# Hyperbolic hops of a graph network in blocks of 64 tiles, with two half chains on VectorE and one set of head buffers

## What is computed

```python
    def _agg(entity_emb, relation_emb, head, tail, relation_type):
        head_emb = entity_emb[head]
        tail_emb = entity_emb[tail]
        rel_emb = relation_emb[relation_type]
        ricci = _l2_normalize(tail_emb + rel_emb)
        hyper_head = expmap0(head_emb)
        hyper_tail = expmap(tail_emb, hyper_head)
        hyper_rel = expmap(rel_emb, hyper_head)
        res = project(mobius_add(hyper_tail, hyper_rel))
        res = logmap(res, hyper_head) + ricci * 1e-07
        res = jax.nn.relu(res)
        sums = jnp.zeros((n_entities, res.shape[-1]), res.dtype).at[head].add(res)
        ...
    for _ in range(N_HOPS):
        e = _agg(e, relation_emb, head, tail, relation_type)
        e = _l2_normalize(e)
        entity_res_emb = RES_LAMBDA * entity_res_emb + e
```

## Time and profile before

| | |
|---|---|
| median of 3 runs | 24083.2 us (24078.12 to 24092.08) |
| the profiled execution | 24039.33 us, its span 24037.5 us |
| first hop, and second hop with the end | from about 16471 us; from about 20276 us |
| VectorE busy, of the span | 16546.3 us (69%) |
| GpSimd busy, of the span | 12605.7 us (52%) |

### The profile page before, as it was taken

One profiled execution on the slowest core, in us unless ns is written; L12 is line 12 of the kernel. 1 busy time (PEld: TensorE's weight loads), 2 busy tenths in 40 slices (PEclk: granted clock), 3 DMA queues, 4 the chain that ended last, 5 costly groups with the idle time before them and its releaser, 6 DMA issues. The chain is left out here.

```text
span 24037.5 us, 205919 instructions
## 1 busy us (share of the span) xinstructions
PE 10326.4 (43%) x47565; PEld 6860.3 (29%) x47566; DVE 16546.3 (69%) x26071; ACT 2139.0 (9%) x3670; POOL 12605.7 (52%) x12782
## 2 busy tenths in 40 slices
PE   0033326655555555556666422222333333333333
PEld 0033322222222222222222322222333332333332
DVE  8744439988888888886666211115888886878887
ACT  0011110000000000000000000001111111111111
POOL 0188876655566555536665166653444443444443
PEclk9999997555555555558887555555555555555555
DMA  4133331111111111121112001113111112111112
GB/s 170 25 69 69 69 64 25 24 23 23 22 21 23 23 23 23 22 20 24 24 24 23 9 21 21 21 21 49 52 51 50 51 50 41 52 51 50 52 50 42
DMA packets 1118452, 942.42 MB, mean 39 GB/s; under 512 B 775931, under 2 KB 887579, under 8 KB 1117875
## 3 DMA queue, kind: packets, MB, share of 16 engines
q0 software_dynamic: 419904, 437.84, 9.9%
q1 hardware_dynamic: 698096, 500.67, 8.0%
HBM read 726.46 MB, written 207.32 MB: 39 GB/s over the span
## 5 line engine op out<-in xcount | busy, mean ns | idle before, releaser
L1420 POOL DMA_INDIRECT tail<-ball,h_idx x3328 | 3271.7, 983 | 1793.3 <-issue 1231.1
L736 PE MATMUL p_rad<-w_stack,hid_t 99*128 99x512 bf16 (+1 forms) x6656 | 3079.6, 620 | 2391.3 <-DVEq L826 1161.0
L808 DVE TENSOR_REDUCE red<-prod 128x96 f32<-128x1536 f32 x1664 | 2898.3, 1742 | 3.5
L1098 POOL DMA_INDIRECT l_xg<-h_tab,l_idx x1664 | 1571.2, 944 | 1444.1 <-issue 828.3
L1452 PE MATMUL h_sum<-head,h_hot 128*128 128x64 f32 x6656 | 1444.2, 421 | 1987.4 <-ACT head L1498 1987.4
L1438 PE MATMUL h_head<-ball_parts,hot_t 128*128 x9984 | 1067.6, 281 | 2813.4 <-issue 1578.1
L337 POOL DMA_INDIRECT rec_a<-rec,slot x1600 | 1990.4, 1244 | 517.2 <-issue 500.5
L692 POOL DMA_INDIRECT rec_b<-l_rcb x1600 | 1920.0, 1200 | 571.6 <-issue 570.5
L930 POOL DMA_INDIRECT l_xg<-x_tab,l_idx x1664 | 1571.6, 944 | 1141.8 <-issue 874.0
L946 PE MATMUL l_sum<-outer,l_hot 128*128 128x512 f32 x3328 | 1693.3, 673 | 945.6 <-DVEq L991 869.7
L736 PEld LDWEIGHTS p_rad<-w_stack,hid_t 99*128 99x128 bf16 (+1 forms) x6656 | 774.5, 132 | 4337.7 <-issue 4336.0
(11 more groups left out here) (369 smaller groups left out, 18896.7 us busy)
## 6 DMA issues: line engine op xcount, KB each, us to landing
hot_t<-rows_l SPq DMA_DIRECT2D x208, 512.0 KB
rec_a<-fill SPq DMA_DIRECT2D x128, 728.0 KB, 19.6
l_rec<-rec_a SPq DMA_DIRECT2D x104, 896.0 KB, 4.8
rhot_t<-rows_r SPq DMA_DIRECT2D x208, 384.0 KB
tail<-ball,h_idx POOLq DMA_INDIRECT x3328
t<-in_type SPq DMA_DIRECT2D x100, 500.0 KB
l_xg<-in_x,l_idx POOLq DMA_INDIRECT x1664
l_xg<-x_tab,l_idx POOLq DMA_INDIRECT x1664
```

Source lines behind the costliest of these rows:

```text
L736: ins = pe.matmul(p_rad[j % 2][:, h * 512:(h + 1) * 512], hid_t[j // 4 % 2][0:K3 + 3 * (1 - i), j % 4, i, :], w_stack[i][0:K3 + 3 * (1 - i ...
L808: ch.step(dve.tensor_reduce(red[:, j, :], prod[j % 3][:, :, :], AX, ALU.add))
L1420: pool.indirect_dma_start(tg[q][:, j, :], None, table[:, :], bass.IndirectOffsetOnAxis(ap=idx[q][:, j:j + 1], axis=0)).then_inc(gathered[q ...
```

## The change

A block becomes 64 tiles (`W` = `HU * BT`, four units of 16), so a hop has 26 blocks. On VectorE each operation of the chain is written twice, once per half block of 32 tiles, and waits for the operation before last instead of the last. To make room, `head`, `rel` and `t_dot_r` are held once instead of twice, the one-hot of the sum is two buffers of 8 tiles, `p_rel` is one bank, and the lists of nodes, lanes and relations go to DRAM and come back block by block. Therefore TensorE picks the heads of block b+1 after the sums of block b; the map words are read during the sums (`words`). ScalarE signals each copy by itself. GpSimd gathers a unit as soon as that unit is released. Outside the hops, `x_kept` is stored in `norm_phase` and read back, the halved entity sum goes through DRAM between the hops (`ent_kept`), and the semaphores of two earlier phases are shared and cleared at their end.

```diff
+HU = 4
...
-        W, Q, H = 2 * BT, BT // 2, BT // 4
+        W, Q, H, N2 = HU * BT, HU * BT // 4, BT // 4, HU * BT // 2
+        HP8 = BT // 2
...
-        hg = [sb(f"head{q}" + tag, [P, W, T_PICK]) for q in range(2)]
-        rg = [sb(f"rel{q}" + tag, [P, W, D + 2]) for q in range(2)]
+        hg = sb("head" + tag, [P, W, T_PICK])
+        rg = sb("rel" + tag, [P, W, D + 2])
...
+            def rows(b, u):
+                h = u % 2
+                hold(sp, turn, picked, (b * HU + u) * H + (AHEAD - H))
...
+            def body(b, q, it, left):
+                rows(b, 0)
+                rows(b, 1)
+                if left:
+                    hold(sp, turn, tails_read, b + 1)
+                    lists(b + 1, 1 - q)
+                    hold(sp, turn, ends_used, b + 1)
+                    edge_ends(b + 1, 1 - q)
+                rows(b, 2)
+                rows(b, 3)
...
-                    hold(pool, turn, tails_used, b + 1)
-                    ch.do(pool.tensor_copy(idx[q][:, :], g["dst_b"][:, bass.ds(b * W, W)]))
+                    hold(pool, turn, idx_in[q], it * 16 + 16)
                     for j in range(W):
+                        if j % BT == 0:
+                            hold(pool, turn, tails_used, b * HU + (j // BT + 1))
...
             def body(b, q, it, left):
-                if left:
-                    pick(b + 1)
                 hold(pe, turn, added, b + 1)
+                chunk = []
                 for j in range(W):
                     if j % BT == 0:
...
+                        if left:
+                            chunk.extend(words(b + 1, j // BT))
+                        hold(pe, turn, relu_done, b * HU + (j // BT + 1))
+                    if j % HP8 == 0:
+                        hold(pe, turn, edge_hot, b * (2 * HU) + (j // HP8 + 1))
+                    ins = pe.matmul(p_sum[:, j // 2, :], hot[j // HP8 % 2][:, j % HP8, :], hg[:, j, 0:D], start=(j % 2 == 0), stop=(j % 2 == 1))
+                    if j % HP8 == HP8 - 1:
                         ins.then_inc(sum_done, 1)
+                if left:
+                    pick(b + 1, chunk)
...
-                act.wait_ge(copied, 2)
-                act.sem_clear(copied)
-                act.sem_inc(taken, 1)
+            def quads(b):
+                for k in range(Q):
+                    hold(act, turn, picked, b * Q + (k + 1 + AHEAD))
+                    act.activation(rg[:, 4 * k:4 * k + 4, :], p_rel[:, :, 0:D + 2], ACT.Copy).then_inc(rel_taken, 1)
+                    act.activation(hg[:, 4 * k:4 * k + 4, :], p_head[k % 2][:, :, 0:T_PICK], ACT.Copy).then_inc(taken, 1)
...
+            def hots(q, b, m):
+
+                z = slice(m * HP8, m * HP8 + HP8)
+                if m >= 2:
+                    dve.wait_ge(sum_done, b * (2 * HU) + (m - 1))
...
-                    z = slice(0, W)
...
-                    ch.sync()
-                    ch.step(f(S, S2, E, B2, z))
+                    for half in range(2):
+                        z = slice(half * (W // 2), (half + 1) * (W // 2))
...
+                        if ch.n > 1:
+                            dve.wait_ge(chain_s, ch.n - 1)
+                        ch.step(f(S, S2, E, B2, z))
...
-                hots(q, b, 0)
+                if left:
+                    compares(b + 1, 0)
+                    compares(b + 1, 1)
...
-                hots(q, b, 1)
+                if left:
+                    relation_hots(1 - q, it + q)
...
+                    for m in range(2):
+                        hots(q, b, 2 * u + m)
+                dve.sem_inc(ends_used, 1)
+                for u in range(HU):
+                    dve.wait_ge(sum_done, b * (2 * HU) + (2 * u + 2))
+                    add_groups(dve, ch, chunk[u * BG:u * BG + BG], acc, lambda k: p_sum[:, u * BG + k:u * BG + k + 1, :])
+                dve.sem_inc(added, 1)
                 if left:
-                    tails(1 - q, b + 1, it + q)
-                    heads(1 - q, b + 1, load_chunks)
...
+                    compares(b + 1, 2)
+                    tails(1 - q, it + q)
+                    compares(b + 1, 3)
+                    heads(1 - q, b + 1)
...
-            store_nodes(sp, x_kept, g["x"], D, stored)
+            w = NT // list_i.shape[1]
+            sp.dma_start(list_i, g["dst_b"][:, :].rearrange("p (b w) -> p b w", w=w)).then_inc(stored, 16)
...
-            norm_phase(nc, g, acc, g["dis"], None, "2", bias=bias)
+            norm_phase(nc, g, acc, g["dis"], x_kept, "2", bias=bias)
...
+            load_phase(nc, tab[:, :, 0:D], x_kept, "0")
```

More of the change, by code:

```diff
@@ L1083, in spread_phase @@
         gathered = [sem(f"l2_gathered{u}") for u in range(4)]
-        row_ready, idx_ready, hot_done, sum_done, added, turn, chain_s = (
-            sem("l2_" + n) for n in ("row_ready", "idx_ready", "hot_done", "sum_done", "added", "turn", "chain"))
+        both = shared(g, ["h_" + n for n in ("row_ready", "idx_ready", "hot_done", "sum_done", "added", "turn", "chain")])
+        row_ready, idx_ready, hot_done, sum_done, added, turn, chain_s = both
+        ctx.callback(clear_shared, nc, both)
         block = ctx.enter_context(nc.Block())
@@ new lines, in pick @@
+            def pick(b, chunk):
+                for k in range(Q):
+                    u, i = k // H, k % H
+                    if i == 0:
+                        hold(pe, turn, hot_done, b * HU + (u + 1))
+                    hold(pe, turn, taken, b * Q + (k + 1))
+                    for j in range(4):
+                        for part in range(3):
+                            pe.matmul(p_head[k % 2][:, j, 0:T_PICK], hot_t[u % 2][:, 4 * i + j, :],
+                                      parts[:, bass.ds(chunk[2 * k + j // 2], 1), part, :], start=(part == 0), stop=(part == 2))
+                    hold(pe, turn, rel_taken, b * Q + (k + 1))
+                    for j in range(4):
+                        ins = pe.matmul(p_rel[:, j, 0:D + 2], rhot_t[u % 2][:, 4 * i + j, :], rel_parts[:, :], start=True, stop=True)
+                    ins.then_inc(picked, 1)
@@ L1454, in body @@
                         ins.then_inc(sum_done, 1)
+                if left:
+                    pick(b + 1, chunk)
             pe.sem_inc(picked, AHEAD)
-            pe.sem_inc(sum_done, SEED)
-            pick(0)
+            pick(0, [c for u in range(HU) for c in words(0, u)])
             all_blocks(pe, NW, body)
@@ L1500, in _ @@
             act.activation(p_row[:, 0:P], g["row"][:, :], ACT.Copy).then_inc(row_ready, 1)
             act.sem_inc(taken, SEED)
-            for k in range(Q):
-                quad(0, 0, k)
+            act.sem_inc(rel_taken, 1)
+            quads(0)
             all_blocks(act, NW, body)
@@ new lines, in with_relation, with tails, heads @@
+            def with_relation(vec, out, u):
+                ch.do(tt(v2[:, :, 0:NREL3], vec[:, unit(u), T_REL:T_REL + NREL3], rhot[:, unit(u), :], MUL_))
+                ch.do(dve.tensor_reduce(out[:, unit(u)], v2[:, :, 0:NREL3], AX, ADD))
+            def tails(q, it):
+                dve.wait_ge(gathered[q], it * (16 * W) + 16 * W)
+                for u in range(HU):
+                    with_relation(tg[q], tr, u)
+                dve.sem_inc(tails_read, 1)
+            def heads(q, b):
+                t = tg[q]
+                for u in range(HU):
+                    z = unit(u)
+                    dve.wait_ge(taken, b * Q + ((u + 1) * H + SEED))
+                    with_relation(hg, sc[:, HV + 1, :], u)
+                    ch.do(tt(v2[:, :, :], hg[:, z, 0:D], t[:, z, 0:D], MUL_))
+                    ch.do(dve.tensor_reduce(sc[:, HV, z], v2[:, :, :], AX, ADD))
+                dve.wait_ge(rel_taken, b * Q + (Q + 1))
@@ L1700, in body, with load_chunks @@
                 big = [P, BT, D]
-                for half in range(2):
-                    z = slice(half * BT, half * BT + BT)
+                chunk = []
+                def load_chunks():
+                    chunk.extend(chunks(dve, g["map"][1], b * (N2 // PACK) + len(chunk) // PACK))
+                for u in range(HU):
+                    z = unit(u)
                     for vec, c in ((h, 16), (t, 18), (r, 19)):
                         ch.step(tt(vec[:, z, 0:D], vec[:, z, 0:D], bc(sc[:, c, z].unsqueeze(2), big), MUL_))
+                    load_chunks()
@@ L1727, in body, with unit_phase @@
                 ch.restart()
-                dve.sem_inc(added, 1)
-            compares(0)
-            tails(0, 0, 0)
+            for u in range(HU):
+                compares(0, u)
+            relation_hots(0, 0)
+            tails(0, 0)
             heads(0, 0)
-            compares(1)
             ch.restart()
             all_blocks(dve, NW, body)
-def unit_phase(nc, g, acc, ent, tab, tag):
+def unit_phase(nc, g, acc, ent, ent_from, ent_to, tab, tag):
     with ExitStack() as ctx:
```

284 lines of the change are left out of this document (127 added, 157 removed).

## The result

The changed kernel took 23944.1 us (median of 4 runs, 23927.7 to 23970.5) beside 24087.6 us of the kernel before: a ratio of 0.994, 95% interval 0.9923 to 0.9958. It is 143 us faster, where 628 were forecast, and lies outside the range. Later sets of runs fell on other chips, and there the same two kernels stood at 0.9587 (0.9571 to 0.9603), 974 us apart, outside the range on its other side. What follows explains both.

What follows compares the result with a forecast made beforehand. VectorE was taken to set the hops' pace: 114.4 us of work plus 11.9 of waiting make 126.3 per 64-tile block, 3372 per hop against 3698. Saving 652 in both hops, less 24 around them, gives 23455 us, range 23120 to 23845.

Steps and rivals of the forecast that it cites:

- Chain: VectorE's chain of dependent operations as two streams: 32.0 us per 64 tiles, the second stream saving 23.7 us.
- Rival 1: In VectorE's chain, two streams gain nothing: a block of 150.0 us, 24689 us in all; chance 7%.
- gaps inside the loop: Extra time of VectorE's chain inside the loop over outside it: 3.2 us per 64 tiles, bounds 0 and 5.
- Rest of VectorE's row: VectorE's work outside the chain per 64 tiles, including vector products 24.6, additions 12.0, heads 16.4 and tails 5.8 us.
- Ends of a hop, and around: First chain 132 us after the hop's start, last block 83 us; stores, loads and semaphore clearing around the hops +24 us.
- The wait that comes in: After the additions VectorE waits 11.9 us per block for rows that need TensorE's picks, now made after its sums.
- R: The moment in a block when VectorE finishes the last unit's vectors, from which the wait for picks is counted.
- lower bound of 6: Shortest wait for picked rows per block, 6 us, with sums ending early, no late copy and no table load.
- no further wait: After the first wait for rows, VectorE finds unit 3's rows and heads ready, with 5 us to spare.
- idle times of 0 or 24 us: Sign in the profile: VectorE idle this long before a block's second L1552, instead of some 12 us, refutes the hand-over sum.
- rival 2: The hand-over of picks costs twice as much, 24 us a block, ScalarE being late: 138.3 us, total 24057; chance 3%.
- its half, 132 to 137 us: Half the extra hand-over cost: a block of 132 to 137 us, 23750 to 24000 us in all; chance 10%.

Runs made afterwards that it cites:

- e18: The changed kernel, unaltered, run again on a chip with signals on time: 22570.0 us, 0.9586 of the kernel before.
- e4: Changed kernel with each chain operation waiting for the one just before it instead of the last but one: 23678.4 us, 1.0057 of the kernel before.
- e7: The kernel before, unaltered, profiled on a chip with signals on time: 23555.0 us (one run).
- e5: The changed kernel, unaltered, on a chip with signals on time: 22580.7 us, 0.9587 of the kernel before.
- sets 3 and 4: Two sets of follow-up runs, each on its own chip, with late signals; the kernel before took 24060.0 and 24040.2 us there.
- e11: The kernel before with four additional ScalarE copies ahead of each quad's copies, as a delay: 24234.7 us, 1.0075 of the unaltered kernel before.
- sets 1, 2 and 5: Three sets of follow-up runs, each on its own chip, with signals on time; the kernel before took 23545.2, 23554.9 and 23541.4 us.
- e15: Changed kernel with the gathers of tails left out in both hops, on a chip with late signals: 22741.1 us (one run).

## Why the prediction was wrong, step by step

From one block of each profile (e18 from 17546.30 on, the first profile from 18008.87 on), and the hops:

| term, us | forecast | on time (e18) | late (first profile) |
|---|---|---|---|
| chain with two comparisons and relation one-hot | 37.9 | 35.1 | 34.2 |
| vectors, words, eight one-hots | 37.4 | 37.0 | 37.3 |
| additions | 12.0 | 11.8 | 11.7 |
| waits for picks | 11.9 | 5.3 | 15.2 + 6.0 + 6.5 |
| comparisons, tails, heads, trip of the loop | 27.1 | 29.3 | 26.3 |
| period, mean of 25 | 126.3 | 117.0 | 136.4 |
| start of the hop to the first chain | 132 | 128.9 | 126.9 |
| last body | 83 | 82.0 | 82.0 |
| around the hops | +24 | +21 | +40 |

- **Chain**: the mechanism right, the size 2.8 to 3.7 us too large. Rival 1 is refuted by e4: the second stream is worth 21.2 us of the 23.7 forecast. The 3.2 us for gaps inside the loop were too many: no gap of that kind is in either block.
- **Rest of VectorE's row**: right to within 1 us; the 29.3 holds a trip of 3.25 where I had the mean of 1.6.
- **Two slips in the sum**: 19.6 us of heads less 2.4 for the words is 17.2 and not 16.4, and R + 19.2 with 7.1 for the rows is R + 26.3 and not R + 26.6; together half a microsecond a block, without weight.
- **Ends of a hop, and around**: right. Around the hops it is 1002.3 us (both hops, e7 to e18) less 981.4 (spans) = 21. In the first comparison both hops shrank by 149.9 us and the rest grew by 40, since the first hop began 27.8 us later; of that the on-time pair shows 8.6, and on chips with late signals this start lies anywhere from 16460.9 to 16512.8 in nine profiles, those of the first comparison included.
- **The wait that comes in**: this step failed, and in it the price of a quad.

  On time, with R at 17615.3: sums end at R + 8.6 (9.9 forecast), unit 0 is picked at R + 13.6 (19.2), as a quad takes 1.24 us (1.45), with no table load and no late copy; rows land 6.6 us after the issue (7.1). The wait is 5.3 us. It is 6.6 us less than I had, 3.5 of them the table load and the late copy, charged for nothing where signals are on time.

  It also lies under my lower bound of 6, which had kept 1.45 us for a quad; with my own lower price of 0.9 that sum gives 8.4 + 3.6 + 7.1 - 14.7 = 4.4.

  The spans of e7 and e18 are 981 us apart, 353 more than forecast: the changed kernel's two hops took 6260.7 us and not 6744, 483 less (330 for the wait, 140 for the chain, the rest small), but on such a chip the kernel before has hops of 7263.1 and not 7396, 133 less.

  Late, with R at 18077.3: sums end at R + 8.8, but unit 0 is picked at R + 24.3. The rows of unit 3, issued 13.3 us after those of unit 2 where I had 5.8, bring the second wait, and the heads of unit 3 the third; for both I had written "no further wait". Waits of 27.8 us for 11.9, and a chain shorter by 3.7, make the main part of 136.4 against 126.3; the two hops took 7247.1 us, 503 more than forecast. I had set idle times of 0 or 24 us, in place of 12, as signs against my sum for the hand-over; it is 15.2 at that place and 27.8 with the two waits behind it, so the sum is refuted. It is what rival 2 describes, and the 136.4 us lie in its half, 132 to 137 us, which I had at 10 in 100.

The row that would have told it stood in the earlier trace rows: 489.7 us of late copies in 80 waits. I took from it one example of 2.46 us and charged it once a block. It is a price per quad: 489.7 / 51 = 9.6 us in 32 tiles, 19 in 64, harmless as long as the quads ran beside the chain. Moved behind the sums, sixteen of them belonged into the sum, with 10 to 20 us in place of 2.2; that gives a block of 134 to 144 (an estimate, made after the result), and 136.4 was measured.

## What to carry to other kernels

When a change moves work from beside the bound onto the path, price it again from its own waits, per piece, and above all the waits whose releaser the profile does not name: they cost nothing where they were. Two interleaved streams of short dependent VectorE operations halved the time of a pair (0.45 to 0.23 us) and took the chain (L1618 to L1745, with the comparisons in it) from 56.1 us in e4 to 34.9 in e5, with one changed wait. Where a kernel signals from TensorE beside indirect gathers, time it on several chips, and keep the gathers out of a stretch in which many such signals follow one another.

## What the runs showed of the hardware

- On the chips of the first comparison and of sets 3 and 4 TensorE's signals come late while GpSimd's gathers are in flight, by 2.28 us in the mean in the first profile and by 2.1 to 2.7 in the others, up to 10.8 (e11); on those of sets 1, 2 and 5 the same program has them on time (0.04 us in the mean in e5 and e18), but for two in a hundred that are over 0.2 us late, one by 8.7 (e7). The kernel before takes 24040 to 24088 us on the former and 23541 to 23555 on the latter, 2%. Why chips differ is not known. Of the 492 signals of the first profile that are over 0.3 us late, 240 rise between the eighth gather of a group and the first of the next, while GpSimd waits for the group to land, and none rises later than 2.1 us after the end of the last gather's issue. This fits a signal that is held back at the longest until the gathers under way have landed; what holds it is open.
- The Trainium skill's "Perfetto Trace Analysis", section "Tensor Engine Instruction (MATMUL, LD_WEIGHTS)", says that the profiler estimates the end of a matmul. In e15 the semaphore rises 0.01 us after that estimated end in all 832 quads, so the estimate is not what makes 2.28 us elsewhere, and the two receivers at 18101.45 and 18101.55 show the lateness without it. Whether the write into PSUM or only the signal is late, the trace can't tell.
- ScalarE's first copy after Relu comes without a table load in the changed kernel (none stands before L1505 at 18089.44), where the earlier trace rows had one of 1.28 us. Why is not shown.
